# A two-layer decoder on Trainium2: the score maxima of the second attention enter through a row of the queries, and TensorE gets products that nobody reads

## The reference, cut to what matters

```python
st = jnp.einsum('bthd,bshd->bths', Qt, Kt)
ss = jnp.einsum('bthd,bshd->bths', Qs, Ks)
score = jnp.concatenate([-sig * st, ss], axis=2) * SCALE
attn = jax.nn.softmax(score, axis=-1)
ctx = jnp.einsum('bths,bshd->bthd', attn, V).reshape(B, T, D)
```

## Time and profile before

| | |
|---|---|
| median of 3 runs | 2300.03 us |
| lowest and highest | 2291.24 and 2302.69 us |
| the profiled execution | 2291.94 us, its span 2290.1 us |
| TensorE, products | 1903.2 us busy, 83% |
| VectorE | 1672.3 us, 73% |
| ScalarE | 1120.7 us, 49% |
| GpSimd | 843.9 us, 37% |
| granted TensorE clock, mean | 0.916 of full speed |

### The profile page before, as it was taken

One profiled execution on the slowest core, in us unless ns is written; L12 is line 12 of the kernel. 1 busy time (PEld: TensorE's weight loads), 2 busy tenths in 40 slices (PEclk: granted clock), 3 DMA queues, 4 the chain that ended last, 5 costly groups with the idle time before them and its releaser, 6 DMA issues.

```text
span 2290.1 us, 39869 instructions
## 1 busy us (share of the span) xinstructions
PE 1903.2 (83%) x14136; PEld 1361.8 (59%) x14136; DVE 1672.3 (73%) x4099; ACT 1120.7 (49%) x3181; POOL 843.9 (37%) x766
## 2 busy tenths in 40 slices
PE   3885698888897898788897898788897889787798
PEld 2564367755685567655685567646684568565464
DVE  8986895679847894679747994789667994735355
ACT  5561366436652556336642566346643565244343
POOL 1551463327512662327421651337431751311000
PEclk8997899989997999889997999899997999788799
DMA  4000011302040012202040012101040203233000
GB/s 147 1 1 10 14 61 30 108 10 75 1 130 18 18 58 79 59 10 74 6 127 15 27 48 88 50 22 63 6 132 11 74 1 119 92 100 102 10 15 24
DMA packets 72491, 116.56 MB, mean 51 GB/s; under 512 B 7822, under 2 KB 46870, under 8 KB 71782
## 3 DMA queue, kind: packets, MB, share of 16 engines
q1 hardware_dynamic: 66758, 100.90, 13.8%
q0 software_dynamic: 5536, 13.12, 1.9%
HBM read 94.66 MB, written 18.28 MB: 49 GB/s over the span
## 4 chain that ended last, share of the span: by engine, by line
DVE 38%; PE 36%; issue 12%; POOL 5%; ACT 5%; DMA 2%; SPq 1%; DVEq 0%; POOLq 0%; ACTq 0%
PE bank L1515 33%; DVE work L516 12%; DVE bank L525 5%; DVE work L514 4%; ACT work L1048 3%; DVE work L534 3%; POOL hid L1416 2%; DVE max L831 2%; PE bank L1519 1%; DVE norm_t_st L446 1%; POOL work L1396 1%; DVE norm_x_st L446 1%; DMA hid<-y_sorted,slot_id 1%; DVE acc L737 1%; POOL work L1391 1%
## 5 line engine op out<-in xcount | busy, mean ns | idle before, releaser
L1515 PEld LDWEIGHTS bank<-work 128*128 128x128 f32 (+2 forms) x5152 | 388.7, 200 | 170.7 <-issue 163.8
L1515 PE MATMUL bank<-work 128*128 128x128 f32 (+2 forms) x5152 | 420.6, 308 | 53.1 <-DMA work<-in_wo 25.2
L1048 ACT ACTIVATE work<-bank 128x512 f32<-128x512 f32 (+1 forms) x560 | 247.0, 519 | 295.7 <-PE bank L1515 263.7
L516 DVE TENSOR_TENSOR work<-bank,table_space 64x512 f32<-64x512 f32 x512 | 352.2, 688 | 6.8
L1384 POOL TENSOR_TENSOR work<-work 128x512 f32<-128x512 f32 x128 | 163.6, 1278 | 398.2 <-PE bank L1515 319.4
L1048 ACT ACTIVATE work<-work 128x512 f32<-128x512 f32 (+1 forms) x338 | 196.6, 618 | 119.0 <-DVE work L604 81.0
L1048 ACT ACTIVATE work<-work,negmax 128x128 f32<-128x128 f32 x512 | 199.1, 390 | 99.6 <-DVE negmax L536 99.6
L1391 POOL TENSOR_TENSOR work<-sb_ident,nrm 128x512 f32<-128x512 f32 x128 | 133.3, 1041 | 201.3 <-ACT nrm L1048 200.5
L1048 ACT ACTIVATE hid<-bank,w_ring 128x128 f32<-128x128 f32 x480 | 136.4, 370 | 132.5 <-PE bank L1515 132.4
L1515 PE MATMUL bank<-work,table_space 128*128 128x512 f32 x256 | 140.5, 630 | 65.9 <-DVE negmax L536 58.0
L514 DVE TENSOR_TENSOR work<-bank,table_space 128x512 f32<-128x512 f32 x256 | 173.7, 678 | 27.0 <-PE bank L1515 21.4
(11 more groups left out here) (296 smaller groups left out, 3378.3 us busy)
## 6 DMA issues: line engine op xcount, KB each, us to landing
w_ring<-in_w_routed SPq DMA_DIRECT2D x120, 514.0 KB, 4.6
x_quad<-x_sorted SPq DMA_DIRECT2D x24, 256.0 KB, 2.9
y_sorted<-y_quad SPq DMA_DIRECT2D x24, 256.0 KB, 4.3
x_T<-in_x_T POOLq DMA_DIRECT2D x9, 256.0 KB, 3.2
x_row<-in_x_row POOLq DMA_DIRECT2D x9, 256.0 KB, 3.8
ctx_T<-in_ctx_T SPq DMA_DIRECT2D x8, 256.0 KB, 2.7
work<-in_ctx_row SPq DMA_DIRECT2D x8, 256.0 KB, 3.0
out<-act_row SPq DMA_DIRECT2D x8, 256.0 KB, 2.3
```

The lines of the kernel that those rows point to most:

```text
L516: last = v.tensor_tensor(rows(wk[i + 1][o]), rows(src[p]), sinT[o, s].unsqueeze(1).broadcast_to([DH0, GB, N]), ALU.mult)
L1048: return nc.scalar.activation(o, i, f, **k)
L1515: return nc.tensor.matmul(o, l, r, start=start, stop=stop, skip_group_check=True)
```

## The change

The maxima no longer go through bf16 parts. `max2` becomes two tiles of 512 columns in the work space, one for slots 0 and 1, one for 2 and 3, cleared by POOL (`clear_max`) before each second attention. DVE writes each maximum into the column that becomes, after the transposition, a row of its own quarter that the slot does not use (`max_col`): 16 and 17 for slots 0 and 1, 0 and 1 for slots 2 and 3. `turn_max` now transposes 128 rows. `less_max(i)` takes bank 7 from q2 in one operation; the second result overwrites q2. The masked keys get a 1 in that row, through a bias of ACT's (`max_row`, function Identity in place of Copy). So the scores of `scores2` also contain one row of q2, the same for all keys, and the scores of `scores2_T` contain the row less the maximum; the row cancels. The four selector products of each `scores2_T` are gone. And `keep_clock(k)` puts k products of 128 x 128 by 256 columns into bank 6, which nothing reads, at four places of TensorE's list.

```diff
-        slot_mask = cols[:, 16:16 + SLOTS]
+        slot_mask, max_row = cols[:, 16:16 + SLOTS], cols[:, 16 + SLOTS:16 + 2 * SLOTS]
...
-        max2 = sb("max2", 128, GB, SLOTS, QUADS)
-        m2_parts = [m_parts, sb("m2_parts", 72, W, dtype=bf16)]
+        max2 = [wk[i].rearrange("p (b r c) -> p b r c", b=GB, r=QUADS) for i in (10, 12)]
+        max_col = (2 * DH2, 2 * DH2 + 1, 0, 1)
         q2, k2, ctx2, rden2 = wk[0], [wk[1], wk[2], wk[3], wk[16]], hid[1], wk[17]
+        q2_less = [wk[17], q2]
...
-                v.memset(m2_parts[1][:], 0.0)
...
-                def split_max(i):
-
-                    P = m2_parts[i]
-                    rest_of = rden2[0:8, :]
+                def less_max(i):
+
                     dve.wait_ge(mx2_T, g * 2 + i + 1)
-                    link(v.tensor_copy(P[0:8, :], bank[7][0:8, :]))
-                    link(v.tensor_tensor(rest_of, bank[7][0:8, :], P[0:8, :], ALU.subtract))
-                    link(v.tensor_copy(P[32:40, :], rest_of))
-                    v.tensor_tensor(P[64:72, :], rest_of, P[32:40, :], ALU.subtract).then_inc(mx2_sb, 1)
-
+                    v.tensor_tensor(q2_less[i], q2, bank[7][:], ALU.subtract).then_inc(mx2_sb, 1)
+
+                dve.wait_ge(max2_clear, g + 1)
                 for n in range(SLOTS):
                     dve.wait_ge(s2, g * SLOTS + n + 1)
                     for r in range(QUADS):
-                        v.tensor_reduce(max2[:, :, n, r], rows(ring2[(4 * n + r) % 6]), X, ALU.max).then_inc(mx2, 1)
+                        v.tensor_reduce(max2[n // 2][:, :, r, max_col[n]], rows(ring2[(4 * n + r) % 6]), X, ALU.max).then_inc(mx2, 1)
...
-                    fn(k2[n], bank[5][:], ACT.Copy, scale=slot_mask[:, n:n + 1]).then_inc(k2_masked, 1)
+                    fn(k2[n], bank[5][:], ACT.Identity, bias=max_row[:, n:n + 1],
+                       scale=slot_mask[:, n:n + 1]).then_inc(k2_masked, 1)
...
+            def clear_max():
+
+                q.memset(wk[10], 0.0)
+                q.memset(wk[12], 0.0).then_inc(max2_clear, 1)
+
...
                 if d:
                     q.memset(work[:, 18 * W:22 * W], 0.0).then_inc(v2_clear, 1)
+                    clear_max()
...
             q.memset(work[:, 18 * W:22 * W], 0.0).then_inc(v2_clear, 1)
+            pool.wait_ge(h_done, BLK + AHEAD)
+            clear_max()
             attn1(G - 1)
...
                     for b in range(GB):
-                        last = nc.tensor.transpose(rows(bank[7][0:8])[:, b],
-                                                   max2[:, b, 2 * i:2 * i + 2].rearrange("p n r -> p (n r)"), ident[:])
+                        last = nc.tensor.transpose(rows(bank[7])[:, b], max2[i][:, b].rearrange("p r c -> p (r c)"),
+                                                   ident[:])
...
-                    for r in range(QUADS):
-                        mm(ring2[(16 + 4 * n + r) % 6][:], sel24[:, (n % 2) * 4 + r], m2_parts[n // 2][:], stop=False)
                     for b in range(GB):
                         for r in range(QUADS):
                             rr = slice(32 * r, 32 * r + 32)
-                            last = mm(rows(ring2[(16 + 4 * n + r) % 6])[:, b], rows(k2[n][rr])[:, b], rows(q2[rr])[:, b],
-                                      start=False)
+                            last = mm(rows(ring2[(16 + 4 * n + r) % 6])[:, b], rows(k2[n][rr])[:, b],
+                                      rows(q2_less[n // 2][rr])[:, b], start=b == 0)
...
+                def keep_clock(k):
+
+
+                    for _ in range(k):
+                        mm(bank[6][:, 0:2 * N], ident[:], seq_T[:, 0:2 * N])
+
                 scores2(0)
                 if more:
                     tokens_T(g, 1)
                     router_logits(g, 1)
+                keep_clock(2)
                 scores2(1)
+                keep_clock(3)
                 scores2(2)
                 turn_max(0)
+                keep_clock(2)
                 scores2(3)
+                keep_clock(3)
                 scores2_T(0)
                 turn_max(1)
                 scores2_T(1)
...
     cols[:, 16:20] = i[:, None] % 32 // DH2 == np.arange(SLOTS)
+    cols[:, 20:24] = i[:, None] % 32 == (2 * DH2, 2 * DH2 + 1, 0, 1)
```

More of the change, by code:

```diff
@@ L196, in decoder @@
         attn_out, ctx_read, v2_clear = sem("attn_out"), sem("ctx_read"), sem("v2_clear")
+        max2_clear = sem("max2_clear")
         half_down = sem("half_down")
@@ L834, in attn1 @@
                     if n == 2:
-                        split_max(0)
-                split_max(1)
+                        less_max(0)
+                less_max(1)
                 if more:
```

## The result

The changed kernel takes **2207.53 us** (median of 4 runs, 2202.56 to 2213.72) against 2295.64 for the kernel before on the same chip (4 runs, 2284.45 to 2302.69). The ratio is 0.9622, with a 95% interval of 0.9572 to 0.9671. The forecast was 2220 with a range of 2205 to 2245. The profiled execution took 2208.61 us, with a span of 2206.8.

A forecast was written before the change was run, and what follows sets the result against it. The prediction took a TensorE-DVE chain at half product speed in the second attention as the bound. Savings of 59.4, 8.4 and about 10.1 us (77.9) from 2291.94 gave 2214, adjusted to a 2220 median; range 2205 to 2245.

The forecast's parts named there:

- mark 8: First second attention, scores2_T(2): without its selector products (0.97) it ends 9.3 us earlier than before, at 478.1.
- rival A: The forecast case: unread products hold the full clock; 2214 by the sum, 2220 taken for the median; chance 0.82.
- B: Unread products don't hold the clock and cost 0.96 each; -2.4 us a block, 19 in all, 2273; chance 0.12.
- the rule behind B: Trainium skill: transpositions don't count as PE-busy the same way; if identity-weight products were taken so, 2273 in place of 2214.
- Marks 1 to 7: First second attention, scores2(1) to heads2(0): full-clock times, from +0.25 us at scores2(1) to -8.3 at heads2(0)'s end.
- Mark 9: First second attention, token_ranks: arrives before its operand, ready at 478.3; a new wait of 0.3 us cuts the gain to 9.0.
- The sum over eight blocks: All second attentions: six save 9.9 us each (59.4), the fifth 8.4, the last about 10.1; 77.9 in all.
- From 2214 to 2220: Profiled execution to median: old median stood 8 above, giving 2222; less sensitivity with a held clock, so 2220.
- All this hangs on 1.00 in the block: Second attention: the forecast saving was said to depend on TensorE's full clock (2.4 GHz) throughout the block.
- GpSimd's clearings: POOL's two clearings ahead of the second attention: 0.9 to 3.6 us together, hidden under 14.07 us of idleness.
- C: Slower: half clock holds to the block's end, the last stretch runs +10.0 us, net +7.6 a block, 2353; chance 0.03.
- D: Block ends sooner but the next group waits as much for a transfer or POOL; 2292, no change; chance 0.03.

The follow-up runs named there:

- The run with 32 rows: The changed kernel, but each unread product takes 32 rows of the identity and operand in place of 128; 2252.23 us, 0.9814 of the kernel before.
- that with transpositions: The changed kernel with each unread product replaced by four unread 128 x 128 transpositions; 2211.17 us, 0.9640 of the kernel before.
- the free row alone: The changed kernel without its unread products: maxima go through an unused row of the queries, no split or selector products; 2229.77 us, 0.9715 of the kernel before.

## Why the prediction was right

The sum came to 2214 for the profiled execution, which took 2208.6; 2220 was given for the median, which came at 2207.5, near the lower end of the range. By the marks, with the first score product of block 1 laid on that of the kernel before (2.49 us later now; mark 8, scores2_T(2), is not apart from its neighbours in the trace):

| mark | forecast | measured |
|---|---|---|
| 1 scores2(1) end | 464.15 | 464.10 |
| 2 scores2(2) start | 465.64 | 465.60 |
| 3 maxima of slot 2 | 466.86 | 466.83 |
| 4 less_max(0) end | 470.03 | 469.91 |
| 5 scores2_T(0) start | 471.47 | 471.26 |
| 6 scores2_T(1) start | 473.93 | 473.72 |
| 7 heads2(0) start | 475.10 | 474.82 |
| 9 token_ranks start | 478.3 | 477.96 |
| 10 last operation | 488.77 | 488.25 |

- **The clock (rival A against B)** held, 1.00 in every block, as the likeliest case had it. The run with 32 rows shows B's course, and that with transpositions that the rule behind B did not act here. The gaps ahead of the old fall were a little longer than the rows let me say: the trace has one of 0.69 at 460.96 beside the 0.58.
- **Marks 1 to 7** were right to within 0.3 us. The first products are a mis-sized term: 0.52 each, not 0.48. It cost nothing at mark 1, since the router's logits ended a little sooner, nor at mark 2, where scores2(2) still starts 1.44 after the maxima of slot 1 (466.65 to 468.09).
- **Mark 9 was wrong.** The new wait of 0.3 did not come. The operand was there at 480.09 + 0.21 = 480.30, 477.81 on the scale of the table and not 478.3, because less_max(1) was through 0.4 sooner, and TensorE came to it at 480.45. So the block lost 10.4 us and not 9.9. That the wait is real and near is seen in the free row alone, where it is 0.48.
- **The sum over eight blocks** was 77.9 against 78.9, with an error in it that was hidden: five ordinary blocks gave 10.5 each for 9.9, the fifth 9.0 for 8.4, the last 10.1 for 10.1, but the seventh only 7.4 for 9.9. I had taken it as an ordinary one that only lacks the queries; the gaps in its last products, which the kernel before does not have, take 2.8 of the difference (3.9 for 1.06). Two mistakes of opposite sign made the sum look better than its terms.
- **From 2214 to 2220** was the worst step. I gave back 8 us because the median before stood 8 above its profiled execution, and took 2 off for the clock. The median after stood 1.1 below. Those 8 us came from three runs; with the fourth the median before is 2295.64, 3.7 above the profile. So most of what I gave back was the scatter of a few runs. Whether the half-clock stretches make the rest was not shown: the runs still spread over 11 us after the change, and over 15 when it was run again.
- **"All this hangs on 1.00 in the block" was too strong.** 65 of the 87 us came from the free row, at a mean clock of 0.79 in its second block. In rival B I had priced the products' cost at half clock, but never the change without them; that case would have shown it.
- **GpSimd's clearings** cost 0.54 each (the lower end, a quarter of 1.82, would be 0.46) and ACT's four masks with a bias about 0.1 more each (2.78 us for the four, 2.42 before); both stayed hidden. C and D did not occur: no window of a block reads below 1.00, and the seven stretches between blocks did not grow in all (1381.8 us against 1387.3), though one of them did, from 215.4 to 219.7.

## What to carry to other kernels

Price a change of two parts three times: both, and each without the other. Here the shorter chain was worth three quarters, and the unread products, by holding the clock, the rest. If narrow products run in the waits of a chain, look at the clock column there even where TensorE's busy share is near full; a few unread products of all rows in waits that exist anyway can hold it, but count them out: two fewer lost about 10 us, ten more lost 32. And don't carry the excess of a median of three runs over its profiled execution to the new kernel.

## What the runs showed of the hardware that I had not expected

- TensorE busy 10.00 of 10.00 us, nearly all with score products and unread ones of 32 rows, stayed at 0.50 (1.2 GHz); with the unread ones at 128 rows the same lists had 1.00 (2.4 GHz).
- Transpositions of 128 x 128 held 1.00 as well as plain products did: 29.64 us a block against 29.77.
- Unread products are cheaper in a row (0.40 to 0.43 for each further one) than the 0.52 of two or three between groups of scores.
- In the last products of the seventh block TensorE stands idle for 0.3 to 1.0 us at a time with no releaser named, with DMA busy (346 GB/s) or not (33). The cause is open.
